# Three-part products of a graph layer, regrouped by part within each block of work

## The reference

```python
d = (sum(adj, axis=1) + 1e-9) ** -0.5
msg_f = (d[:, None] * adj * d[None, :]) @ x            # and the same with spatial_x
H_f = relu(msg_f @ W_f + b_f);  H_s = relu(msg_s @ W_s + b_s)
a = sigmoid(concat(H_f, H_s) @ W_att + b_att)
out = layernorm(x + a * H_f + (1 - a) * H_s)
```

## Time and profile before

| | |
|---|---|
| median of 3 runs | 401.71 us |
| the profiled execution: its own time | 402.25 us |
| its span, from first to last instruction | 400.3 us |
| PE busy | 373.3 us, 1748 matmuls, of them 1584 of the split products |
| DVE busy | 291.6 us |
| ACT busy | 284.8 us |
| POOL busy | 141.3 us |
| DMA | 132.86 MB, mean 332 GB/s |

### The profile page before, as it was taken

One profiled execution on the slowest core, in us unless ns is written; L12 is line 12 of the kernel. 1 busy time (PEld: TensorE's weight loads), 2 busy tenths in 40 slices (PEclk: granted clock), 3 DMA queues, 4 the chain that ended last, 5 costly groups with the idle time before them and its releaser, 6 DMA issues. The chain is left out here.

```text
span 400.3 us, 5279 instructions
## 1 busy us (share of the span) xinstructions
PE 373.3 (93%) x1748; PEld 311.7 (78%) x1748; DVE 291.6 (73%) x401; ACT 284.8 (71%) x349; POOL 141.3 (35%) x189
## 2 busy tenths in 40 slices
PE   1789799999999999999979999999999999999990
PEld 2668578888888888788868888888788888888990
DVE  2586484978687856969389765857966796888895
ACT  3776788788878887887887878578533566677565
POOL 1200002572157104650169300003100417877764
PEclk9999999999999999999998999999999999999996
DMA  7999999999999999999999999999655524344011
GB/s 303 396 423 419 424 421 417 420 424 420 421 421 418 424 415 421 422 421 420 421 422 420 422 412 416 417 413 387 221 211 206 212 106 156 160 175 142 21 35 52
DMA packets 25659, 132.86 MB, mean 332 GB/s; under 512 B 2976, under 2 KB 7840, under 8 KB 11424
## 3 DMA queue, kind: packets, MB, share of 16 engines
q1 hardware_dynamic: 25632, 132.53, 82.1%
HBM read 130.42 MB, written 2.10 MB: 331 GB/s over the span
## 5 line engine op out<-in xcount | busy, mean ns | idle before, releaser
L383 PE MATMUL sums<-Ah,Yh 128*128 128x512 f32 (+1 forms) x528 | 204.4, 387 | 9.9 <-DVE Yl L482 5.3
L471 DVE TENSOR_TENSOR Al<-raw,Ah 128x2048 fp32r<-128x2048 f32 (+1 forms) x70 | 156.1, 2234 | 78.9 <-ACT Ah L646 71.5
L385 PE MATMUL sums<-Al,Yh 128*128 128x512 f32 (+1 forms) x528 | 202.7, 384 | 0.0
L384 PE MATMUL sums<-Ah,Yl 128*128 128x512 f32 (+1 forms) x528 | 202.6, 384 | 0.0
L646 ACT ACTIVATE Ah<-raw 128x2048 fp32r<-128x2048 f32 (+1 forms) x70 | 123.4, 1768 | 51.4 <-DMA raw<-in_At 27.9
L383 PEld LDWEIGHTS sums<-Ah,Yh 128*128 128x128 f32 x528 | 99.6, 189 | 31.9 <-DVE Yl L482 6.3
L659 ACT ACTIVATE nat<-nat 128x2048 f32<-128x2048 f32 x53 | 101.7, 1919 | 26.9 <-DMA nat<-in_adj 25.6
L385 PEld LDWEIGHTS sums<-Al,Yh 128*128 128x128 f32 x528 | 99.6, 189 | 19.7
L384 PEld LDWEIGHTS sums<-Ah,Yl 128*128 128x128 f32 x528 | 99.7, 189 | 19.2
L493 DVE TENSOR_TENSOR acc<-sums,acc 128x512 f32<-128x512 f32 (+1 forms) x106 | 66.3, 671 | 6.9 <-PE sums L385 6.9
L759 POOL TENSOR_SCALAR dg<-rs 128x1 f32<-128x1 f32 x22 | 15.5, 703 | 120.4 <-ACT nat L659 120.3
(11 more groups left out here) (49 smaller groups left out, 141.8 us busy)
## 6 DMA issues: line engine op xcount, KB each, us to landing
raw<-in_At SPq DMA_DIRECT2D x63, 1024.0 KB, 10.4
nat<-in_adj SPq DMA_DIRECT2D x48, 1024.0 KB, 12.0
nat<-in_adj SPq DMA_DIRECT2D x8, 768.0 KB, 13.6
xs<-in_xs SPq DMA_DIRECT2D x7, 512.0 KB, 12.2
nat<-in_adj SPq DMA_DIRECT2D x8, 256.0 KB, 10.9
out<-xs SPq DMA_DIRECT2D x32, 64.0 KB, 1.8
raw<-in_At SPq DMA_DIRECT2D x4, 256.0 KB, 10.0
xs<-in_xs SPq DMA_DIRECT2D x1, 384.0 KB, 9.2
```

The costliest lines, as they stand in the source:

```text
L383: pe.matmul(to, Yh[:, t % YRING, hs], high, start=first, stop=False)
L384: pe.matmul(to, Yl[:, t % YRING, hs], high, start=False, stop=False)
L385: mm = pe.matmul(to, Yh[:, t % YRING, hs], low, start=False, stop=last)
L471: dve.tensor_tensor(Al[:, k % SPLITS, a * IB:b * IB], raw[:, k % RAWS, a * IB:b * IB], Ah[:, k % SPLITS, a * IB:b * IB], ALU.subtract).the ...
```

## The change

Nothing is computed otherwise; the same instructions are put in another order on PE and DVE, and PE's waits are split.

- `sweeps` now gives (block, half, product) steps. In items without a beginning or ending run: all Yh*Ah products of the item, then all Yl*Ah, then all Yh*Al. In the others: group by group (a group is the blocks of one run; in items 0 and 1 one block) Yh*Ah and Yl*Ah, and the Yh*Al products of a group two groups behind (`behind`), or, where no run ends, behind all groups. The last two items keep their order.
- PE waits for `Ah` and `Yh` before an item's first product, for `Yl` before its first Yl*Ah, and for `Al` before its first Yh*Al, no longer for all of them at the start.
- On DVE, where four runs ended in item k-1, two of them are evacuated ahead of `Al` of item k and the other two right behind it. Before, two of them came ahead of `Al` of item k+1 and two behind. `Yl` of the tiles below 24 moves ahead of `Al` of the same item.

```diff
     def sweeps(k):
...
+        blocks = range(len(items[k]))
+        tiles = [(e, t == runs[e][1][0], t == runs[e][1][-1]) for e, t in items[k]]
+        if k >= K - 2:
+            return [(j, half, p) for half in range(2) for j in blocks for p in range(3)]
+        begins, ends_runs = any(f for e, f, l in tiles), any(l for e, f, l in tiles)
+        if not begins and not ends_runs and k not in PIECED_ITEMS:
+            return [(j, half, p) for p in range(3) for j in blocks for half in range(2)]
+        if k in PIECED_ITEMS:
+            groups = [[j] for j in blocks]
+        else:
+            groups = [[j for j in blocks if items[k][j][0] == e] for e in dict.fromkeys(b[0] for b in items[k])]
+        behind = 2 if ends_runs or k in PIECED_ITEMS else len(groups)
+        order = []
+        for i in range(len(groups) + behind):
+            if i < len(groups):
+                order += [(j, half, p) for p in range(2) for j in groups[i] for half in range(2)]
+            if behind <= i:
+                order += [(j, half, 2) for half in range(2) for j in groups[i - behind]]
         return order
...
             for k in range(K):
-                pe.wait_ge(Yl_ok, max(t for e, t in items[k]) + 1)
-                if k >= PIECED:
-                    pe.wait_ge(low_ok, GT * (k + 1))
+                newest = max(t for e, t in items[k]) + 1
...
+                    split = GT * k + j + 1 if k in PIECED_ITEMS else GT * (k + 1)
+                    if p == 0 and newest > y_high_seen:
+                        pe.wait_ge(Yh_ok, newest)
+                        y_high_seen = newest
+                    if p == 0 and split > high_seen:
+                        pe.wait_ge(high_ok, split)
+                        high_seen = split
+                    if p == 1 and newest > y_low_seen:
+                        pe.wait_ge(Yl_ok, newest)
+                        y_low_seen = newest
+                    if p == 2 and split > low_seen:
+                        pe.wait_ge(low_ok, split)
+                        low_seen = split
...
                 ended = [e for e in evac_order if end_item[e] == k - 2]
                 ending = [e for e in evac_order if end_item[e] == k - 1]
-                if k < 2 * G:
-                    evacuate_new(ended[:3])
-                    evacuate_new(ending[:1])
-                elif len(ended) == GT:
-                    evacuate_new(ended[:2])
+                if len(ending) == GT:
+                    evacuate_new(ending[:2])
                 if k == 1:
                     own_share(3)
+                for r in y_at[k]:
+                    if r >= PIECED and r < FULL:
+                        y_low(r)
                 low(k)
+                if len(ending) == GT:
+                    evacuate_new(ending)
                 for r in y_at[k]:
-                    if r >= PIECED:
+                    if r >= FULL:
                         y_low(r)
```

More of the change, by code:

```diff
@@ L20 @@
 PIECED = 2
+PIECED_ITEMS = range(PIECED)
 WARM = 10
@@ L100, in build @@
     for k in range(K):
-        for j, half in sweeps(k):
+        for j, half, p in sweeps(k):
             e, t = items[k][j]
-            if t == runs[e][1][-1]:
+            if t == runs[e][1][-1] and p == 2:
                 done_no[e, half] = len(done_no) + 1
@@ L106, in build @@
                 end_item[e] = k
-        j, half = sweeps(k)[-1]
+        j, half, p = sweeps(k)[-1]
         e, t = items[k][j]
@@ L374, in _, with product @@
         def _(pe):
-            def block_of(k, j, half):
+            def product(k, j, half, p):
                 e, t = items[k][j]
                 g, tiles, pair, (a, b) = runs[e]
-                first, last = t == tiles[0], t == tiles[-1]
                 to = sums[:, pair, half, 0:b - a]
@@ L381, in block_of @@
                 cols = slice(j * (b - a), (j + 1) * (b - a))
[L382 to L385, removed]
+                y = (Yh, Yl, Yh)[p]
+                part = (Ah, Ah, Al)[p]
+                last = t == tiles[-1] and p == 2
+                mm = pe.matmul(to, y[:, t % YRING, hs], part[:, k % SPLITS, cols],
+                               start=t == tiles[0] and p == 0, stop=last)
                 if last:
@@ L435, in _ @@
             started = set()
+            y_high_seen = y_low_seen = 0
             for k in range(K):
-                pe.wait_ge(Yl_ok, max(t for e, t in items[k]) + 1)
-                if k >= PIECED:
-                    pe.wait_ge(low_ok, GT * (k + 1))
+                newest = max(t for e, t in items[k]) + 1
                 due = group_at(k, 1)
-                for step, (j, half) in enumerate(sweeps(k)):
-                    if due == TAIL - 1 and step == len(items[k]):
+                high_seen = low_seen = GT * k
+                for step, (j, half, p) in enumerate(sweeps(k)):
+                    if due == TAIL - 1 and step == 3 * len(items[k]):
                         weigh(due)
-                    if k == K - 1 and step == GT:
+                    if k == K - 1 and step == 3 * GT:
                         weigh_half(HALVES[0])
-                    if k < PIECED and half == 0:
-                        pe.wait_ge(low_ok, GT * k + j + 1)
+                    split = GT * k + j + 1 if k in PIECED_ITEMS else GT * (k + 1)
[11 more added lines that the diff above has]
+                        low_seen = split
                     e = items[k][j][0]
@@ L452, in _ @@
                             pe.wait_ge(evac_ok, 2 * (same_pair_before(e) + 1))
-                    mm = block_of(k, j, half)
+                    mm = product(k, j, half, p)
                 if last_signal[k][0] == "early":
```

## The result

| | before | after |
|---|---|---|
| median of 8 runs each, on one chip | 401.91 us | 404.31 us |
| lowest and highest | 401.68, 402.32 | 403.01, 406.13 |
| profiled execution, own time | 402.25 | 405.74 |
| its span | 400.3 | 403.7 |
| item 48 starts (profiled execution) | 288.71 | 292.15 |

The ratio of the times is 1.006, with a 95% interval from 1.0035 to 1.0085: slower by 0.6%, or 2.4 us. The forecast was 403.1, the range 401.4 to 405.4. The eight times of the changed kernel stand in two groups: 403.01, 403.08, 403.33, 403.53, and 405.09, 405.24, 405.74, 406.13. The profiled execution belongs to the upper one. In the ratios further down, times more than 1.5% above the fastest of the same kernel are left out, which happens in run 2 alone, to two of its twelve.

A forecast was written before the change was run, and what follows sets the result against it. PE alone bounds from item 48 on, whose start is set by item 47's landing, then ACT, DVE and PE. Terms 0 + 0.9 + 0.5 = +1.4 us on the 401.71 us median gave 403.1 us, range 401.4 to 405.4.

The forecast's parts named there:

- Of the early gain 0 us passes this point: At item 47, PE arriving up to 5.3 us early still waits for DVE's evacuation at 285.8; 0 us gained.
- Four matmuls more: In item 47, 16 matmuls instead of 12 stand behind the awaited evacuation: +0.9 us.
- The gap in the DMA stream: Load of item 22, issued after `Al` of item 19, comes late; gap 0.5 - g + c, 0 to 2.6, taken +0.5 us.
- g: How much earlier than 118.19 us item 18 starts on PE: 0 to 2.6 us, taken as 1.
- c: Extra time of `Al` of item 19 on DVE beside POOL's sums: 0 to 2.1 us, taken as 1.
- Each us of gap goes into the landing of item 47: With the DMA stream full to the stage's end, any gap delays item 47's landing in full; +0.5 us taken.
- The clock before item 47: Rival: PE idles twice around item 47 and drops to half speed, up to +1.7 us, 404.8 us; chance 0.24.
- Faster, because landings follow the earlier `Al`: Rival: loads issued earlier after `Al` of items 11, 15, 35 land items 47 and 48 earlier; -1.8, 399.9 us; chance 0.09.
- The grown gap: Rival: late `Al` in items 10/11 and 18/19 both meet POOL; gap 2.6, total +3.5, 405.2 us; chance 0.09.
- The pitch of the matmuls: PE's 0.227 us per matmul, assumed unchanged though consecutive matmuls now change PSUM bank; taken as 0.

The follow-up runs named there:

- run 2: Changed kernel, with DVE's late evacuations in items 46 and 47 moved ahead of `Al` or right behind it: 399.36 us, ratio 0.9931.
- run 3: Kernel before the change, with only DVE's evacuations in items 46 and 47 moved ahead of `Al` or right behind it: 401.29 us, ratio 0.9967.
- run 4: Changed kernel plus 19 matmuls into an unused bank, filling PE's two waits at item 47: 404.03 us, ratio 1.0052.
- run 1: Changed kernel, with item 47's own product order put back so 12 matmuls, not 16, stand behind the wait: 402.99 us, ratio 1.0038.
- run 5: Only PE's part of the change, with DVE in the order of the kernel before: 405.52 us, ratio 1.0088.
- run 10: Changed kernel with run 2's move, and in items 14 to 30 DVE does `Al`, two evacuations, next `Al`, two evacuations: 397.2 us, ratio 0.9877.
- run 7: Changed kernel, with all four evacuations of ended runs put behind `Al` on DVE: 403.93 us, ratio 1.0049.
- run 12: Changed kernel plus four small matmuls adding zeros in item 4: 405.35 us, ratio 1.0066.
- run 9: The kernel of run 8 plus four small matmuls adding zeros in item 4: 400.15 us, ratio 0.9956.
- run 6: Only DVE's part of the change, with PE in the order of the kernel before: 411.1 us, ratio 1.0227.
- run 8: Changed kernel with run 2's move, and all four evacuations behind `Al` on DVE from item 8 on: 401.28 us, ratio 0.998.

## Why the prediction was right, and where a term was mis-sized

- **"Of the early gain 0 us passes this point."** Shown. PE was done with item 46 some 3 us earlier and waited for the same chain of landing, ACT and DVE. Run 2 took that chain's last link away and the time fell by 5 us (404.31 to 399.36). Not all of this is early gain: the wait's own costs, the clock's 1.7 and the 0.9, went with it. Against the kernel before it is 2.7 us, of which run 3's move alone gives 0.8.
- **Four matmuls more, +0.9.** It is seen in run 4 by 16 matmuls in 3.76 us where 12 had taken 2.87, and run 1 fits it (0.6 to 1.3 us came back).
- **The gap in the DMA stream, +0.5 with g = 1 and c = 1.** The place held, the size did not, and that the sum came out near is in part luck. Item 18 started at 116.6, so g was 1.6; `Al` of item 19 ended at 126.1, so c was 1.6, and 0.5 - g + c is 0.5 again. But the stream lost 1.2 us there, and 0.8 more in a hole at 105 us that the sum hasn't: 2.0 us, where the forecast had 0.5. The bytes still lag by 2 us at 275 us (412 GB/s on average up to there, where the kernel before has 415), so nothing filled the holes. Yet `Ah` of items 27 and 34 starts 2.3 and 2.4 us late, of items 41 to 46 1.6, and of item 47 only 0.8. Item 47 lands with fewer bytes moved ahead of it than before; which ones, and why, is open. "Each us of gap goes into the landing of item 47" is the step that didn't hold. Runs 5 and 10 against the changed kernel show that the hole at 127 comes from DVE's order.
- **The clock before item 47, a rival at 0.24, +1.7.** This is the term that was mis-sized most. The forecast's sum gives it nothing. In the profiled execution it cost its full 1.7. The prediction had put PE's arrival and both waits there (2.3 us or more and 2.7; measured 2.79 and 1.78), so the chance was too small, not the price. With the landing's 0.8 and the matmuls' 0.9 alone, the time would be 401.9 + 1.7 = 403.6, next to the lower group; with the clock 405.3, in the upper one. Runs 4 and 7 are on the two sides of it in their profiles. That each of the four low times of the changed kernel itself is an execution without the fall is argued, not shown. The mean granted clock of each execution fits it (0.986 to 0.988 in the lower group, 0.982 to 0.986 in the upper). It is plainer in run 12, where nothing falls at item 5: 0.991 in its one low time (402.9) and 0.986 to 0.988 in the five others.
- **Faster, because landings follow the earlier `Al`** (0.09). Refuted: they came later. **The grown gap** (0.09) had its price of 2.6 us for holes at items 10/11 and 18/19. In the changed kernel's profile the first of them is missing (422 GB/s in the 9th slice, 81 to 91 us). In the profiles of runs 1 and 2, which have the same orders up to there, both are there and a third between them, and `Ah` of item 47 starts 5.2 and 3.2 us late. So this rival is real in some executions, and its price was too small.
- **The pitch of the matmuls**, named as a risk outside the range: unchanged. 24 matmuls take 5.44 us in run 10.

The Trainium skill ("TensorE: Matmul & The Clock Gate", Part 1) calls half speed the default from which activity releases the engine. The trace agrees in so far as the waits of item 47 and of item 5 of the changed kernel were followed by half speed. That sentence doesn't tell which waits cost it: in run 9, waits of 2.26 and 2.36 us were followed by full speed.

## What to carry to other kernels

Before an earlier start is counted as a gain, follow it to the next place where the engine waits for a chain it does not belong to: here all of it ended at an evacuation whose time was set by a landing, and it came through only when that evacuation was moved. An instruction put earlier on one engine ties what stands behind it to another engine, and the loads that wait for the latter can leave a hole in a full DMA stream, which nothing later fills here. An engine that arrives early just waits longer, and on TensorE a longer wait right before the stage that it bounds can cost more than it saved.

## What the runs showed of the hardware

- The granted clock fell after short waits, but not after all of them. Among others, it fell behind waits of 1.81 and 2.79 us (changed kernel, items 5 and 47), 2.22, 2.54 (run 6), 2.56 (run 8, item 10) and 2.66 (run 3, item 5). It stayed at 1.00 behind 2.70, 2.05 (run 7, item 34), 2.20 (run 5, item 34), 2.26 and 2.36 (run 9), 1.90 (run 8, item 34), 1.49 (run 3, item 34) and 2.74 (run 12, item 47, though it fell behind the next wait, of 2.34). The length of the wait alone does not decide. Each fall ahead of the last stage lasted 3.4 us, and the one in item 47 of the changed kernel 6.8.
- A load of 1 MB into a queue that was nearly dry took 4.9 us (issued 126.15, landed 131.1), where the earlier trace rows had 4.7 in the quiet stage. The Trainium skill ("DMA: Bandwidth & Descriptors", Anatomy of one DMA) gives a fixed cost of some 2.0 us and 436 GB/s for DMAs that GpSimd issues; by this, as an estimate, 4.4 us. Here SyncE issues them, and the measurement decides.
- `Al` took 2.29 us alone and up to 3.38 beside POOL's sums, `Yl` 0.48 and 1.32. Of two that overlapped, the one that began second was the longer, and the first kept its time: in the changed kernel POOL's sum at 122.69 took 1.28 us and `Al` at 122.75 3.38; `Al` at 116.92 took 2.28 and POOL's sum at 116.93 3.43, where 1.30 is its usual time.
- A single program's times scattered by 3.1 us in the changed kernel, 7.4 in run 2 and 5.3 in run 5, and by 0.9 in runs 7 and 10, of which five and four executions were timed. How much of it is holes and how much the clock, and why both come out so unlike from one execution to the next, is open.
